# Graph network kernel: TensorE waits for each tile's own gather, and makes the next layer's table one chunk behind each tile of a step's last group

## The reference, cut to what matters

```python
h = relu(layernorm(x))
x = x + segment_sum((h * src_norm)[src], dst) * dst_norm          # layer 0
h = relu(layernorm(x))
for l in range(2):                                                # layers 1 and 2
    seg = dst * 65 + edge_type
    mean = segment_sum(h[src], seg) / max(count(seg), 1)          # per node and type
    conv = relu(einsum('nrd,rdk->nk', mean, W[l]) + h @ root[l] + bias[l])
    h = conv + relu(h @ res_W[l] + res_b[l])
x = x + h
```

## Time and profile before

| | |
|---|---|
| median of 3 runs | 14958.47 us (14957.38 to 14958.64) |
| the profiled execution | 14875.71 us, span 14873.9 us |
| PE busy | 5800.3 us, 39% of the span |
| DVE, ACT busy | 5235.7 us (35%), 1745.6 us (12%) |
| POOL busy | 9176.7 us, 62% |
| mean granted clock of TensorE | 0.649 of full speed |
| mean share of the DMA engines' time in the gathers' queue | 11.3% |

### The profile page before, as it was taken

How to read it: one execution, slowest core, us unless ns; L and a number is a source line. 1 busy time by engine, 2 the same in 40 slices (tenths; PEclk the granted TensorE clock), 3 DMA queues, 4 the chain that set the end, 5 groups by cost and what they waited for, 6 DMA issues and landing times.

```text
span 14873.9 us, 133991 instructions
## 1 busy us (share of the span) xinstructions
PE 5800.3 (39%) x30700; PEld 4202.1 (28%) x30700; DVE 5235.7 (35%) x19301; ACT 1745.6 (12%) x4604; POOL 9176.7 (62%) x9689
## 2 busy tenths in 40 slices
PE   5443434343433434344444434444333333333333
PEld 4322222222222222222222222222222232322322
DVE  9655555555555532222222222222112122221122
ACT  7311111111111111111111111111000000000000
POOL 0466666666666656666666666665666666666666
PEclk7666666666666666666666666666556556555565
DMA  1333333333333322222222222221111111111111
GB/s 36 99 118 118 120 116 122 114 125 112 125 115 122 116 92 71 65 71 69 67 69 67 71 68 68 69 67 57 24 24 24 24 24 24 24 24 24 25 24 31
DMA packets 522512, 1049.42 MB, mean 71 GB/s; under 512 B 216194, under 2 KB 248720, under 8 KB 522240
## 3 DMA queue, kind: packets, MB, share of 16 engines
q1 hardware_dynamic: 212832, 729.64, 13.2%
q0 software_dynamic: 309408, 317.45, 11.3%
HBM read 599.09 MB, written 447.31 MB: 70 GB/s over the span
## 4 chain that ended last, share of the span: by engine, by line
another core or an unknown queue 41%; issue 20%; DVE 14%; PE 11%; POOL 7%; DVEq 4%; ACT 1%; DMA 1%; SPq 0%; ACTq 0%; POOLq 0%
POOL rows L495 7%; PE sums_ps L778 5%; PE y_ps L729 5%; DVE scr L924 5%; DVE same_more L924 3%; DVE onehot L914 2%; DVEq L914 2%; DVE ystage L888 1%; DVEq L924 1%; DMA rows<-y_table,idx_st 1%; DVE onehot L916 1%; ACT ystage L614 1%; PE y_ps L734 1%; DVE w_sb L929 0%
## 5 line engine op out<-in xcount | busy, mean ns | idle before, releaser
L495 POOL DMA_INDIRECT rows<-y_table,idx_st x6446 | 6102.0, 947 | 3435.1 <-issue 1984.7
L778 PE MATMUL sums_ps<-onehot,rows 128*64 128x128 f32 (+1 forms) x19338 | 3373.7, 345 | 2929.5 <-DMA rows<-y_table,idx_st 1624.9
L495 POOL DMA_INDIRECT rows<-h_table,idx_st x3223 | 3067.7, 952 | 1781.0 <-issue 942.5
L778 PEld LDWEIGHTS sums_ps<-onehot,rows 128*64 128x64 f32 (+1 forms) x19338 | 3060.5, 182 | 3169.2 <-issue 2178.2
L916 DVE TENSOR_SCALAR onehot<-iota,dst_rel,w_sb 128x128 f32<-128x128 bf16 x6468 | 1716.8, 357 | 6217.7 <-remote 4341.6
L729 PE MATMUL y_ps<-w_parts,hT 128*128 128x512 bf16 (+1 forms) x5400 | 1694.6, 471 | 4541.1 <-ACT hT L600 3161.3
L729 PEld LDWEIGHTS y_ps<-w_parts,hT 128*128 128x128 bf16 x5400 | 570.5, 117 | 5563.0 <-issue 3764.6
L924 DVE TENSOR_SCALAR_CACHE_REDUCE scr<-scr,key_col 128x384 bf16<-128x384 f32 x2352 | 1299.1, 606 | 254.4 <-issue 247.6
L614 ACT ACTIVATE ystage<-y_ps 128x512 f32<-128x512 f32 (+1 forms) x1800 | 998.5, 566 | 1009.8 <-PE y_ps L729 537.9
L590 ACT ACTIVATE idx_st<-pair_i 128x11 int32 (+1 forms) x594 | 124.8, 211 | 8291.3 <-remote 5778.6
L914 DVE TENSOR_SCALAR onehot<-iota,dst_rel 128x128 f32<-128x128 bf16 x3234 | 721.5, 298 | 606.7 <-issue 519.8
(11 more groups left out here) (119 smaller groups left out, 2412.8 us busy)
## 6 DMA issues: line engine op xcount, KB each, us to landing
y_table<-ystage SPq DMA_DIRECT2D x400, 768.0 KB
scr<-key_row SPq DMA_DIRECT2D x297, 832.0 KB
y_table<-ystage SPq DMA_DIRECT2D x200, 608.0 KB
rows<-y_table,idx_st POOLq DMA_INDIRECT x6446
rows<-h_table,idx_st POOLq DMA_INDIRECT x3223
rr<-y_table SPq DMA_DIRECT2D x200, 64.0 KB
w_raw<-in_L_gnn_W SPq DMA_DIRECT2D x4, 1040.0 KB
h_table<-scr SPq DMA_DIRECT2D x2, 1600.0 KB, 11.6
```

The costliest lines, as they stand in the source:

```text
L495: pool.indirect_dma_start(out=rows[:, j, k, 0:D], out_offset=None, in_=table, in_offset=bass.IndirectOffsetOnAxis(ap=idx_st[:, j, k:k + 1] ...
L778: ins = nc.tensor.matmul(sums_ps[u][0:width, c:c + P], rows[:, j, k, 0:width], onehot[:, (J * u + j) % 2, k, :], start=False, stop=False)
```

## The change

Three things change together.

1. **The semaphores of the gathers.** There was one for each layer and group; now there is one for each group and tile, shared by the layers (33 in all). `landed` gives the count to wait for. To have semaphores left for this, nine sets of four on a path that these inputs don't take (`g_idx_ready`, `tile_through` and others) become one each.
2. **PE's waits.** It waited once in a group for all eleven gathers; now each tile's matmul waits for its own gather.
3. **The places of Y.** `h` is still turned behind group 1. Then, in group 2, chunk k - 1 stands behind tile k, for k = 1 to 9. `Y_AFTER` is gone. ACT copies all nine chunks between the stages of groups 1 and 2.

```diff
-        gathered = [[sem(f"gathered{l}{j}") for j in range(J)] for l in range(3)]
+        gathered = [[sem(f"gathered{j}_{k}") for k in range(K)] for j in range(J)]
...
+        def landed(l, s, j, k):
+
+            return 16 * (l * (S - 1 if k >= K - LACK[j] else S) + s + 1)
...
-        Y_AFTER = ((), (0, 1), range(2, YG))
...
-                                .then_inc(gathered[l][j], 16)
+                                .then_inc(gathered[j][k], 16)
...
-                                if l < 2:
-                                    emit_y(l, s, u, i, Y_AFTER[j])
+                                if l < 2 and j == 1:
+                                    emit_y(l, s, u, i)
...
-                            if l < 2 and j:
-                                transform(l, s, Y_AFTER[j - 1][1:])
+                            if l < 2 and j == J - 1:
+                                turn_h(l, s)
                             pe.wait_ge(onehot_ready[l], q + 1)
-                            pe.wait_ge(gathered[l][j], s * (16 * K) + 16 * tiles)
                             for k in range(tiles):
+                                pe.wait_ge(gathered[j][k], landed(l, s, j, k))
                                 c = column_of(j * K + k, T)
                                 ins = nc.tensor.matmul(sums_ps[u][0:width, c:c + P], rows[:, j, k, 0:width],
                                                        onehot[:, (J * u + j) % 2, k, :], start=False, stop=False)
+                                if l < 2 and j == J - 1 and 0 < k <= YC:
+                                    transform(l, s, (k - 1,))
+                            if l < 2 and j == J - 1:
+                                transform(l, s, range(max(tiles - 1, 0), YC))
                             if j == J - 1:
                                 ins = clear_sums(u, D + 1, start=False, stop=True)
                             ins.then_inc(agg_done[l], 1)
                             if j == 0:
                                 turn_block(l, s, u)
-                            if l < 2:
-                                transform(l, s, Y_AFTER[j][0:1])
```

More of the change, by code:

```diff
@@ L192, in gnn_kernel @@
         sums_zeroed = sem("sums_zeroed")
-        tile_through = [sem(f"tile_through{k}") for k in range(4)]
+        tile_through = sem("tile_through")
         edges_loaded = [sem(f"edges_loaded{k}") for k in range(4)]
[L195 to L198, removed]
+        padded = sem("padded")
+        g_idx_ready = sem("g_idx_ready")
+        g_turned = sem("g_turned")
+        g_eq_ready = sem("g_eq_ready")
         g_gathered = [sem(f"g_gathered{k}") for k in range(4)]
-        g_rows_ready = [sem(f"g_rows_ready{k}") for k in range(4)]
-        g_summed = [sem(f"g_summed{k}") for k in range(4)]
-        g_new_ready = [sem(f"g_new_ready{k}") for k in range(4)]
+        g_rows_ready = sem("g_rows_ready")
+        g_summed = sem("g_summed")
+        g_new_ready = sem("g_new_ready")
         block_loaded = [sem(f"block_loaded{l}") for l in range(3)]
@@ L529, in add_tile @@
                         wait_alone(pool, sums_saved[kind], (t + 1) * 16)
[L530 removed]
+                        pool.sem_inc(tile_through, 1)
                     pool.wait_ge(sums_zeroed, 64)
[L533 removed]
+                    pool.sem_inc(tile_through, 1)
                     if kind:
[L535 removed]
+                        pool.wait_ge(tile_through, kind * (TILES + 1))
                     if kind == 1:
@@ L711, in _, with turn_h, transform @@
             turn(3, "pair", f_pair)
[L713 to L722, removed]
+            def turn_h(l, s):
+                pe.wait_ge(h_ready[l], s + 1 + 1)
+                for a in range(2):
+                    ins = nc.tensor.transpose(t_ps[:, a * P:(a + 1) * P],
+                                              h_parts[:, a, :, :].rearrange("p b d -> p (b d)"), ident_b[:, :])
+                ins.then_inc(hT_done[l], 1)
+            def transform(l, s, chunks=None):
+                if chunks is None:
+                    turn_h(l, s)
+                for c in range(YC) if chunks is None else chunks:
+                    if c == 0:
+                        pe.wait_ge(hT_ready[l], s + 1)
                     pe.wait_ge(y_read[l], s * YC + max(c - 1, 0) + 1)
@@ L802, in add_tile @@
                     def add_tile(t):
-                        pe.wait_ge(g_idx_ready[kind], t + 1)
+                        pe.wait_ge(g_idx_ready, kind * TILES + t + 1)
                         nc.tensor.transpose(sums_ps[0][:, 0:P], g_target_b, ident[:, :])\
-                          .then_inc(g_turned[kind], 1)
-                        pe.wait_ge(g_eq_ready[kind], t + 1)
-                        pe.wait_ge(g_rows_ready[kind], t + 1)
+                          .then_inc(g_turned, 1)
+                        pe.wait_ge(g_eq_ready, kind * TILES + t + 1)
+                        pe.wait_ge(g_rows_ready, kind * TILES + t + 1)
                         nc.tensor.matmul(sums_ps[1][:, 0:cols], g_eq, g_rows[:, D + 1 - cols:D + 1],
-                                         start=True, stop=True).then_inc(g_summed[kind], 1)
+                                         start=True, stop=True).then_inc(g_summed, 1)
                     with pe.Fori(0, FULL) as t:
```

28 lines of the change are left out of this document (15 added, 13 removed).

## The result

The changed kernel takes 16,075.65 us (median of 4 runs, 16,052.32 to 16,084.85), the kernel before beside it 14,957.92 (4 runs, 14,951.35 to 14,958.64): a ratio of 1.0746, 95% interval 1.0733 to 1.0758, 1,118 us more. The profiled execution took 16,052.32 us with a span of 16,050.5, against the span of 14,873.9 of before: 1,176.6 us more.

The account below looks back on a forecast made before the run. Bound by POOL's gathers and an interrupting chain PE -> ACT -> POOL; steps of layers 0 and 1 rise to 56.4 us (47.62 plus 8.75), adding 1,421 to 14,876, plus 83 for the median: 16,380 us, range 14,930 to 16,910.

Parts of the forecast that it names:

- The step as a sum: POOL's step is 33 gathers, 41.2 us in every layer, plus two stops in layer 1 and one in layer 2.
- The stops obey the length of the run ahead of them: POOL's stops of 3.27, 5.11 and 6.72 us after 11, 22 and 33 gathers fit 1.6 us plus 0.157 a gather.
- Counts by PE arrive late during a run: PE's counts pass at once until some 6 us into POOL's run, then mostly not before POOL stops.
- A wait for each tile: PE's matmuls each wait for their own gather; priced at zero, at most 4.5 us a step, layer 2 unchanged.
- Round trips ahead of the count: Group 2's count stands behind nine chunks, not six: 2.9 us more, 12.5 us, past the 6 to 8 heard.
- POOL doesn't stop after 22 gathers; it goes on to 33: Layers 0 and 1: group 1 ends 1.7 us earlier, some 7.4 us into the run, and is heard in mid-run.
- the rival of the old pattern: Runs of 11 and 22 gathers stay, only the first stop grows, 4.5 us a step: 15,850 us, chance 0.14.
- The price of the remainder: Chunks left at POOL's stop in layers 0 and 1 cost 11.5, 8.75 or 6.05 us with two, four or six out.
- I take four: Four chunks of Y out before the stop, since layer 2 shows a trickle: remainder 8.75 us, step 56.4 us.
- Of the clock: All-low clock in the remainder would give 10.4 us and about 16,700; the forecast kept a clock that rises inside it.
- "no change" rival: The stops are POOL's own, or holds belong to the profiled execution; time stays 14,958 us, chance 0.15.
- "faster" rival: The nine chunks' round trips are heard, all layers run with one stop: 299 us less, 14,660 us, chance 0.20.

Follow-up runs that it names:

- e10: Changed kernel with chunks 6 to 8 of Y made behind the last group's count: 14,962.92 us beside 14,875.69 for the kernel before, ratio 1.0064.
- e12: Changed kernel with four PSUM buffers of Y in place of two: 15,689.45 us beside 14,879.77 for the kernel before, ratio 1.0548.
- e5: Changed kernel word for word on another chip: 12,723.20 us beside 12,730.90 for the kernel before, ratio 0.9994.
- e9: Changed kernel with 30 more small SP transfers a step: 15,479.14 us beside 14,930.99 for the kernel before, ratio 1.0364.
- e8: Kernel before with 30 more small SP transfers a step: 15,056.89 us beside 14,930.99 without them, ratio 1.0081.

## Why the prediction was right, and where not

The forecast of 16,380 us is 304 above the measured median, 1.9%. Of these, 60 come from how each profiled execution stands to its median (83 us below before, 23 after), and 244 from the sum: 1,421 us forecast, 1,177 in the spans. The profile of before isn't one of the runs of its median. At 14,876 us it is as long as the sets of e10 and e12, so the 83 us can be a difference between sets of runs.

- *The step as a sum: right.* The prediction worked out that without stops the kernel would take 12,700 us. On chips without stops the kernel before takes 12,716, 12,731 and 12,742. Its window of layer 1 began late and has 3,219 of the 3,223 gathers; the layer is 4,796 us, 48.9 a step, not 48.7, and the forecast doesn't use this.
- *"The stops obey the length of the run ahead of them": right on four chips with stops.* Layer 2 has 6.6 to 6.8 us at the median behind 33 gathers in each profile that has stops.
- *"Counts by PE arrive late during a run": right as a fact, too firm as a rule.* "At once until some 6 us" fails in the shown step: group 1 ended 4.5 us into the run and was heard at 21.5. And the rule holds for some chips alone; on the others all counts pass at once (e5).
- *A wait for each tile, priced at nothing: right to the size that was asked.* Layer 2, which has only this edit, takes 4,668 us against 4,641: 0.28 us a step. In e10 tile waits and interleaving together cost 0.6%. They weren't separated on a chip with stops.
- *Round trips ahead of the count, "the cost of the change": right.* With three chunks behind the count the ratio is 1.0064, with none 1.0746 (e10). It was shown on two chips and not on one, but the kernel before differs between these by 0.6% only.
- *"POOL doesn't stop after 22 gathers; it goes on to 33": right in layer 1, wrong in layer 0.* There the rival of the old pattern came true: 390 us over 98 steps are 4.0 us each, where that rival had 4.5. This is the step that failed. Its argument was that group 1's count comes 1.7 us earlier, 7.4 us into the run, and is therefore heard in mid-run. It came 6.0 us into the run in layer 0 and wasn't heard, and 4.5 in layer 1 and was; the prediction had read steps of layers 1 and 2 alone and took layer 0 to be alike. The place in the run doesn't settle it either, since in e9 ten counts of layer 1 at 4.5 us weren't heard: transfers of SP in that stretch go with the old pattern there. Layer 0 has SP's loads of keys, 110 GB/s against 58 in the windows above, so two causes fit there, the later count and the loads. Neither was tried, and the cause stays open.
- *The price of the remainder: right in kind; the number of chunks was wrong.* "I take four" was wrong; two chunks were out. For two the prediction had 11.5 us, and 11.5 was measured at the median (12.7 in the shown step). But it put the remainder on top of layer 2's whole stop of 6.72 us, 59.1 us a step. The first copy came 3.5 us behind POOL's stop, and POOL resumed 1.1 us behind the stage, so only 4.6 us stood beside the remainder, and the shown step was 57.6. So layer 1 rose by 741 us, close to the 715 forecast for it (98 x 7.3), by luck: 2.7 us too little for the chunks and 2.1 too much for the rest of the stop. Most of the sum's error is in layer 0, 390 us where it had 706. e12 confirms the remainder as a cause.

Of the clock, two windows of the shown step, all engines (PE's busy us and count, PEld, DVE, ACT, POOL, then granted clock, DMA share, GB/s):

```profile
7070.80:7079.00 8.20, 6.79 (x17) 2.00 (x18) 0.00 (x0) 2.88 (x5) 0.00 (x0) 0.51 0.23 96
7079.00:7084.00 5.00, 5.00 (x29) 2.43 (x28) 0.47 (x2) 2.64 (x6) 0.00 (x0) 1.00 0.38 157
```

The remainder begins at the low level and ends at the high one, with four chunks in the first window and three in the second. The Trainium skill, page "TensorE: Matmul & The Clock Gate", section "HAM oscillation — how this bites in real kernels", says that a wait for data behind each short burst throws the array back to the low clock every time. That case has long waits for a DMA between its bursts and not the short waits for ACT inside the remainder (0.76 us at 7074.29), so the prediction applied it where it doesn't reach: here the second window is at the high level. With all of it low, two chunks out would be 10.4 + 2 x 1.73 = 13.9 us by the prediction's terms; 12.7 were measured in this step and 11.5, the sum by the rows, at the median.

The "no change" rival is what happens on chips without stops, but not by its mechanism: it had stops that PE can't touch, and there are none. Nor do the holds belong to the profiled execution: it took 16,052 us and the other runs of the changed kernel 16,071 to 16,085. The "faster" rival happened nowhere.

## What to carry to other kernels

A stall can depend on the chip that the program meets: run the kernel before on a second chip before tuning against its waits, and compare where one program's waits end on both. Here the same change costs 7.5% on one chip and nothing on another, so the order that puts fewer round trips between engines ahead of a count that a third engine needs is the safe one. Where a hand-over may be late, what counts is how much work is left behind it: more buffers (2.6 us off the median stop of layer 1 for two more) or moving that work behind the count (6.8 of 7.5 points, between two chips).

## What the runs showed of the hardware

- The kernel before took 14,958, 14,931, 14,876 and 14,880 us on four sets of runs and 12,716, 12,731 and 12,742 on three others, each set within 0.3%. Gathers lasted 948 ns on both kinds. On the first kind counts that PE raises while POOL gathers are heard over 20 us late at worst, and POOL's stops are linear in the gathers ahead of them; on the second neither is seen. What differs between the chips isn't known, nor whether a chip keeps its kind.
- The two kinds can be told from one profile. On the second, part 6 gives 2.4 to 2.5 us to landing for the gathers of layers 1 and 2; on the first it gives none in any profile, and the trace has a fifth of the completions: 34,198 for the changed kernel against 171,929 for the same kernel in e5. That the profile lacks those times where counts are late suggests that the gathers' completion counts are recorded differently too; why wasn't found.
- Thirty more transfers a step, which nearly double the increments, left the stops as they were (e8: 3.4, 5.3, 6.8 us), but went with a layer 1 of the changed kernel in runs of 11 and 22 instead of 33 (e9). That a pause behind each gather would free the counts stays open, since both tries of it met chips of the second kind.
